# Layer norm beside an LSTM's last steps: mean ahead of variance, the mean's subtraction behind the new state

## What is computed

```python
def step(carry, xw_t):                       # L1_cond, 256 positions one after the other
    prev_h, prev_c = carry
    a = xw_t + prev_h @ Wh
    i, f, o = sigmoid(a[:, :H]), sigmoid(a[:, H:2*H]), sigmoid(a[:, 2*H:3*H])
    g = tanh(a[:, 3*H:])
    next_c = f * prev_c + i * g
    next_h = o * tanh(next_c)
    return (next_h, next_c), next_h

# L1_attn: ahead of its projections
mu = mean(h, axis=-1); var = mean(square(h - mu), axis=-1)
xn = (h - mu) * rsqrt(var + 1e-5) * gamma + beta
```

## Time and profile before

| | us |
|---|---|
| median of 3 runs | 2730.02 |
| lowest and highest | 2724.48, 2731.41 |
| profiled execution, its own time | 2729.23 |
| its span | 2727.2 |
| TensorE busy in the span | 2445.4 (90%) |
| VectorE busy | 1926.5 (71%) |
| ScalarE busy | 1156.3 (42%) |
| GpSimd busy | 398.2 (15%) |

### The profile page before, as it was taken

One profiled execution on the slowest core, in us unless ns is written; L12 is line 12 of the kernel. 1 busy time (PEld: TensorE's weight loads), 2 busy tenths in 40 slices (PEclk: granted clock), 3 DMA queues, 4 the chain that ended last, 5 costly groups with the idle time before them and its releaser, 6 DMA issues. The chain is left out here.

```text
span 2727.2 us, 119354 instructions
## 1 busy us (share of the span) xinstructions
PE 2445.4 (90%) x50848; PEld 2042.8 (75%) x50848; DVE 1926.5 (71%) x7414; ACT 1156.3 (42%) x3693; POOL 398.2 (15%) x412
## 2 busy tenths in 40 slices
PE   3678999999999999987768859999999999999999
PEld 1455677777777777654536648999999999999998
DVE  4757777777777777788666656677777776666774
ACT  3225555555555555556346722333333333333333
POOL 0000000000000000000019701222222222222222
PEclk9668999999999999999859958999999999999999
DMA  5000000000000000100013230000000000000000
GB/s 171 1 2 3 5 5 6 5 5 5 5 5 5 5 5 5 36 12 27 4 44 108 77 109 7 9 9 9 9 9 9 9 9 9 9 9 9 5 5 6
DMA packets 53051, 53.66 MB, mean 20 GB/s; under 512 B 24982, under 2 KB 47144, under 8 KB 50602
## 3 DMA queue, kind: packets, MB, share of 16 engines
q1 hardware_dynamic: 47318, 29.70, 4.0%
q0 software_dynamic: 1728, 12.58, 1.3%
q10 hardware_dynamic: 3476, 3.75, 0.5%
HBM read 39.46 MB, written 6.55 MB: 17 GB/s over the span
## 5 line engine op out<-in xcount | busy, mean ns | idle before, releaser
L105 PE MATMUL p<-xn,m_h 128*128 128x128 f16 x6144 | 559.1, 220 | 0.0
L105 PE MATMUL p<-xn,m_l 128*128 128x128 f16 x3072 | 530.3, 220 | 0.0
L105 PEld LDWEIGHTS p<-xn,m_h 128*128 128x128 f16 x6144 | 480.9, 98 | 1.8
L596 PE MATMUL lg_b<-xn,lh 128*32 128x256 f16 x6144 | 303.0, 294 | 85.5 <-DVE lh L1060 77.3
L2119 POOL TENSOR_TENSOR xn<-qkv_w,xn 128x384 f16<-128x384 f32 x256 | 234.3, 915 | 904.5 <-ACT xn L2077 904.5
L1036 DVE STREAM_TRANSPOSE gt<-lg_b 128x512 f32<-128x512 f32 x324 | 230.2, 710 | 187.1 <-PE lg_b L596 184.8
L840 ACT ACTIVATE gl<-gt 128x128 f32<-128x128 f32 x324 | 100.2, 309 | 602.8 <-DVE gt L1036 602.1
L855 ACT ACTIVATE hm<-xy,b 128x512 f32<-128x512 f32 x512 | 347.9, 680 | 0.0
L105 PEld LDWEIGHTS p<-xn,m_l 128*128 128x128 f16 x3072 | 301.1, 98 | 0.7
L2003 PE MATMUL po<-m_h,xn 128*128 128x256 f16 x1536 | 292.6, 272 | 1.9 <-DVE xn L2158 1.9
L596 PEld LDWEIGHTS lg_b<-xn,lh 128*32 128x32 f16 x6144 | 161.1, 102 | 173.3 <-DVE lh L1060 128.8
(11 more groups left out here) (387 smaller groups left out, 6218.2 us busy)
## 6 DMA issues: line engine op xcount, KB each, us to landing
m_stage<-in_m_w POOLq DMA_DIRECT2D x12, 1024.0 KB, 5.2
hs<-in_m_w SPq DMA_DIRECT2D x14, 384.0 KB, 3.2
x_dram<-x SPq DMA_DIRECT2D x16, 128.0 KB, 2.1
xs<-in_l_wv SPq DMA_DIRECT2D x1, 2048.0 KB
attention_dram<-att SPq DMA_DIRECT2D x16, 128.0 KB, 2.8
xn<-x_dram SPq DMA_DIRECT2D x16, 128.0 KB, 2.4
out_dram<-xn SPq DMA_DIRECT2D x16, 128.0 KB, 2.2
xn<-attention_dram SPq DMA_DIRECT2D x124, 16.0 KB, 1.7
```

Of the source, the lines that this page charges most:

```text
L105: ins = pe.matmul(out, w[wp](k), x[xp](k), start=start, stop=last and k == KT - 1 and xp == 1, skip_group_check=True)
L596: last = pe.matmul(gate_block(ae, j, par), lh[:, part, ae, k, u, :], columns(w[name], k, j), start=False, stop=(part == 1 and k == KT - 1) ...
```

## The change

Two calls move, each within one engine's program. On TensorE a unit's mean is issued ahead of the variance of the unit before it. On VectorE the subtraction of the mean is issued behind the three instructions of the LSTM's new state (and behind `norm_low` and the wait for `e_kept`, which have no work in these steps), and ahead of everything else of the slot. No instruction, wait or tile is added or removed.

```diff
@@ -822,10 +822,10 @@
                     project_c(pe)
+                if unit_at(i, slot, 0) is not None:
+                    norm_mean(unit_at(i, slot, 0))
                 if unit_at(i, slot, 1) is not None:
                     norm_var(unit_at(i, slot, 1))
-                if unit_at(i, slot, 0) is not None:
-                    norm_mean(unit_at(i, slot, 0))
                 if pair_at(i, slot, 0) is not None:
                     norm_spread(pair_at(i, slot, 0))
@@ -1319,13 +1319,13 @@
                 cell(i, slot)
                 gather(i, slot)
-                if unit_at(i, slot, 0) is not None:
-                    norm_center(unit_at(i, slot, 0))
                 if pair_at(i, slot, 1) is not None:
                     norm_low(pair_at(i, slot, 1))
                 if slot == E0 and i > LAG:
                     dve.wait_ge(e_kept, 2 * (i - LAG))
                 state(i, slot)
+                if unit_at(i, slot, 0) is not None:
+                    norm_center(unit_at(i, slot, 0))
```

## The result

| | before | after |
|---|---|---|
| median of the runs on one chip, us | 2725.20 (7 runs) | **2716.46** (7 runs) |
| lowest and highest | 2721.86, 2731.41 | 2713.50, 2719.78 |
| profiled execution, its own time | 2729.23 | 2719.78 |
| its span | 2727.2 | 2717.3 |
| ten steps 303 to 312 in it | 45.01 | 35.85 |

The ratio after to before is 0.996, with a 95% interval of 0.9946 to 0.9973: faster, by 0.3 to 0.5%. The three runs of before that the prediction had are among its seven. The medians lie 8.74 us apart, against a predicted 8.8; by the interval the gain is anything from 7.4 to 14.7 us, so that an agreement to 0.1 us is luck.

A forecast was written before the change was run, and what follows sets the result against it. The prediction took a round trip per LSTM step, no engine's throughput, as the bound. Its step terms summed to 36.2 us against 45.0, a gain of 8.8: 2729.23 to 2720.4, plus 0.8 makes 2721.2 us; range 2717.5 to 2727.5.

The forecast's parts named there:

- the last of the sum: Whole time: profiled 2729.23 us less the gain makes 2720.4; taken as 0.8 below the median, so 2721.2.
- faster by over 0.3%: Whole time under 2721.8 us: chance 0.48, four fifths of the forecast's 0.60; within 0.3% had 0.49.
- Mean ahead of variance: TensorE: mean done some 1.0 us behind the transpose, so the subtraction, able to start at 2.41 us, no longer waits.
- Subtraction behind the state, hidden by a hair: VectorE: the 0.60 us subtraction lets the transpose start 1.10 us behind the state; TensorE lets it go at 1.14.
- Step 307: LSTM step with projection quad, mean and variance on TensorE: 2.84 us, then 0.90 for the LSTM's matmuls, 3.8 in all.
- GpSimd's copy in step 303: The moved subtraction lands beside this copy; at worst it pays 0.16 us once, taken as nothing.
- Steps 303 and 305: LSTM steps where VectorE is already last, so the subtraction adds 0.60 us each: 3.82 and 4.14 us.
- Give-back: Step 311: the subtraction starts at 2.41 instead of 1.53 us behind the transpose, so step 312's gates come 0.88 us later.
- The clock: TensorE's clock stays at its upper level up to step 311; waits and order are under half of the 8.8 us.
- The clock alternates where it did: Rival: TensorE slow from 1319.5 to 1326.3 and 1333.1 to 1336.6 us; ten steps 40.5, gain 4.5, 2725.5 us; chance 0.26.
- The clock mattered less behind the median: Rival: in the median's runs the clock cost less than in the profiled one; gain 3.2, 2726.8 us; chance 0.08.
- TensorE becomes the bound: Rival: clock falls in step 304 and stays down; ten steps 51.9 us, 6.9 more than before, 2736.9 us; chance 0.06.

The follow-up runs named there:

- 2x2 table: Ten-step times of old order, mean first, subtraction behind the state, and both; with the clock kept up: 38.70, 36.02, not reached, 35.85 us.
- the one with late fillers: Changed kernel plus matmuls that nobody reads in steps 311 to 322, behind the variance; 2714.87 us, ratio 0.9962, ten steps 36.42 us.
- the kernel that takes it back: Changed kernel with only the last unit's subtraction (step 311) back in front of the new state; 2716.64 us, ratio 0.9965, ten steps 34.97 us.

## Why the prediction was right, and where it failed

**The failed step is the last of the sum**: "The profiled execution took 2729.23 us, so 2720.4; it stands 0.8 below the median, which makes 2721.2." The 0.8 came from three runs (2724.48 to 2731.41). Over seven runs the median of before is 2725.2, so the profiled execution stood 4.0 above it, and the base was 4.8 too high. From 2725.2 the same gain of 8.8 gives 2716.4; measured, 2716.46. And the range took in the errors of the gain but left 0.5 to 0.7 us for "a measurement's spread", though the profile's start of step 303 alone moves by 7.4 us from one execution to the next.

The base alone isn't the whole story. On the chip of the second execution of the changed kernel the median of before was 2729.04 (13 runs), near the predicted base, and that of the changed kernel 2717.21: 11.8 us apart, 3.0 more than the predicted gain (7.9 to 15.6 by the interval). Where that surplus lies isn't shown; the ten steps of that execution, 37.46, don't hold it. The chances for "faster by over 0.3%" and "within", 0.48 and 0.49, compared a gain of 8.8 with a line at 8.2 us and don't hang on the base. The medians give 0.32%, the interval 0.27 to 0.54%, so the line lies inside it.

**Mean ahead of variance**: right. No subtraction of the loop waits for it, and the 2x2 table gives this move 2.68 of the 2.85 us that the order is worth.

**Subtraction behind the state, hidden by a hair**: right. Steps 304, 306, 309, 310 and 311 take 3.04 or 3.05, as predicted; 308 took 3.12, its state 1.98 instead of 1.91 behind the transpose, and no run shows why. In step 309 the mean waited 0.24 us for the subtraction of the unit before (row at 1337.16) and started 0.19 us behind the transpose, not 0.12 ahead of it as the text had it; the step still took 3.04. But the move's worth was small, 0.2 a step in the steps of 3.25, given back in 312. The text costed the two moves together and didn't see that the second, added to the first, brings 0.17 net.

**Step 307**: 3.38, predicted 3.8. The term "-0.12 + 0.8 + 1.11 + 1.05 = 2.84" added the durations of mean and variance as if the next group began at the end of the one before. By the rows above the variance begins 0.97 behind the mean's start (1331.11, 1332.08) and the LSTM 0.88 behind the variance's (1332.96): a group's last matmuls still run while the next one starts. That is 0.31 of the 0.36 us by which the sum before rounding was off.

**GpSimd's copy in step 303**: taken at nothing. The state's third instruction took 0.35 us again, as before, and so the subtraction began 0.67 behind the state instead of 0.50. The subtraction's own duration stayed 0.68, though it overlapped the copy by only 0.04 us (1319.00 to 1319.04). The step took 3.84 against 3.82. By the Trainium skill's "SBUF — State Buffer", section "Who interferes with whom", GpSimd's reads hold up a VectorE instruction with two SBUF inputs, so of these two only the state's third instruction; that agrees, but 0.04 us of overlap is no test of the subtraction's side.

**Steps 303 and 305**: 3.84 and 4.13 against 3.82 and 4.14. Right.

**Give-back**: 0.88 predicted, 0.88 by the kernel that takes it back (6.17 to 5.29). From the subtraction's start at 1345.47 to the gates at 1349.34 it is 3.87 us, as in the earlier trace rows.

**The clock**: right in the profiled execution (1.00 to 1346.8), less so in the other: there the lower level came for 3.4 us from 1324.8, and again from 1341.8, and the ten steps took 37.46. By the Trainium skill's "TensorE: Matmul & The Clock Gate", section "A second HAM failure mode: psum-queue depth-cycling", small idles between groups of matmuls made the clock of another kernel go up and down. The second execution and the one with late fillers agree with it, the first one doesn't. The forecast's "stays up" was too strong: in the executions seen, the new order made the falls rarer and shorter and didn't end them. Why it keeps the clock longer isn't shown beyond that. "Within the 8.8 us, waits and order are worth less than half, the rest is the clock" held: 2.85 of 9.16. That this profile kept the clock up to step 312 was partly luck, by the other one.

**The rivals.** *The clock alternates where it did*, 40.5: no execution of the changed kernel did; the longest took 37.46. *The clock mattered less behind the median*: its sum of 39.4 for the old order at the upper level was tried, 38.70; steps 305, 307 and 309 took 4.91, 4.45 and 3.68 against 4.9, 4.5 and 3.7, and 306 3.25 against 3.7. As a mechanism it isn't borne out: the second profile of before had its low stretch too, 45.56, and fillers shortened the runs without a profile as well, by 6.8 us in the medians. *TensorE becomes the bound*: never. At most two steps in a row met the lower level.

## What to carry to other kernels

In a recurrence, put what the next step doesn't need behind the new state, and order the other engine so that its result is there before it is asked for; check each such move alone, since here the first brought nearly all and the second nearly nothing. Here waits cost twice, as waits (2.85 us in ten steps) and by way of a slower TensorE clock (6.3), and a few matmuls that nobody reads were cheaper than the lower level, where nothing waited behind them. Predict a difference against a base that is measured as often as the result will be, and give that base a width of its own.

## What was not expected of the hardware

- The clock fell at different places in executions of the same program: three times in 45 us in one of before, once, from 1331.4 on for all of the remaining 26.4 us, in the other; not before step 312, and at 1324.8 and 1341.8, in the two of after. A busy TensorE isn't always a fast one: in the low 3.4 us from 1324.8 it was busy for all of it.
- Four matmuls of 128 by 256 columns, 0.60 us, in each of eight steps: with them the old order stayed at 1.00 for 36.5 us, of which TensorE was busy for 28.3. With the subtraction's move alone the clock fell ahead of the first of them.
- The spread of this kernel's whole time sits far from the change: 4.8 us in its first four rounds, 0.4 in the twelve rounds behind them, up to 3.5 from there to step 303, where it goes with the clock, and 4.5 behind step 323.
- Fillers in the first three rounds, where TensorE's granted clock was 0.64 to 0.77, took 11.0 us off the median, more than the 8.74 us of the change itself.
